# Written-out step lists for the first three batches and the last two in a five-engine software pipeline

## The chip, the cores and the metric

The kernel runs on one NeuronCore of a Trainium2 chip. The metric is the device time of one execution in microseconds (us), from its start to its end. Engines are named as in the profile: PE is TensorE, DVE is VectorE, ACT is ScalarE, POOL is GpSimd, SP is SyncE, whose queue issues most DMAs.

## The reference, cut to what matters

For each of 16 sequences ("batches") of 512 tokens with 128 channels the reference computes two layers. The first is an RWKV block and a soft decision tree:

```
x = ln(x); xn = ln(x); xk, xv, xr = mixes of xn and xn shifted by one token
k = exp(min(xk @ Wk, 60)); v = xv @ Wv; r = xr @ Wr
wk, wkv = scan over the tokens of k and k*v with a decay per channel
x = x + (sigmoid(r) * wkv / wk) @ Wo
x = x + sigmoid(xr2 @ cWr) + silu(xk2 @ cWk) @ cWv
x = ln(x); gates of 255 tree nodes; 256 leaf probabilities; x = ln(x + leaves @ values @ Wout)
```

The second is causal attention with 16 heads of 8 channels and rotary angles, and a mixture of 16 experts with the two largest gates, plus shared experts:

```
q, k = rope(rms(x) @ Wq), rope(rms(x) @ Wk); v = rms(x) @ Wv
x = ln(x + softmax(q k^T / sqrt(8), causal) @ v @ Wo)
x = ln(2 x + shared(x) + sum over the experts of gate_e * (x @ We))
```

The passes of one batch depend on one another nearly everywhere: time mix, channel mix, tree, rope, row maxima of the scores, scores and exponentials, attention output, routing, experts.

## The kernel before, in words

Every pass of a batch is cut into steps, each a few instructions of one engine with the semaphore waits that they need. In the file they are small functions: `row_scores` (steps `row0` to `row39`, PE), `row_maxima` (`rowmax0` to `rowmax39`, DVE), `scores` (`score0` to `score39`, PE), `score` (`exp0` to `exp39`, ACT), `weigh` (PE), `rope_product` (`rope0` to `rope3` on PE, `rope_mul0` to `rope_mul3` on DVE), `inverse` (DVE, the reciprocal of line 695), `read_out` (PE), `spread_gate` (`gb`), `expert` (PE), `gated_input` (`u`, even experts on DVE, odd ones on POOL, with ACT's `spread`).

A batch works in 40 score units. The row maxima come first: PE writes a unit into one of two PSUM banks, DVE reduces it (lines 745 and 748). When all are there, the maxima go through `max_parts`, a turn by PE and a DMA into extra rows of `qh`; then PE makes the units again, transposed and shifted by the maxima, and ACT takes the exponential (line 500). `prob` has ten slots; `weigh` frees them.

Rope's outputs are split into three bf16 parts each (`part_hi`, `part_mid`, `part_lo`). `spread_heads` (steps `heads0` and `heads1`, line 313) brings them by 18 DMAs for each half of the heads from `part` into `qh` and `kh`; `row0` of a batch waits for the first half.

Each engine runs in its own program order. The order is a hand-written cyclic list, `ORDER`: an entry `2:row5` in it means that in turn t the engine does `row5` of batch t-2. `run` repeats the list for turn 0, 1, 2 and so on, and leaves out what would fall on a batch below 0 or above 15. So at the start and at the end a turn has the same order as in the middle, with holes where there is no batch. A turn has the row maxima and the channel mix of one batch, the time mix of the next one, and the scores and experts of the one before.

Some constants are prepared inside batch 0's steps: the step `weights` on DVE (lines 854 to 902), PE (lines 1201 to 1206) and ACT (lines 615 to 623) scales, transposes and fuses weight matrices. PE's seventh transpose waits for DVE's first six instructions there, and all that PE has behind `weights`, `read_out0` of batch 0 first, waits for its end.

Two waits matter below. The time mix works in four chunks of 128 hidden channels with two slots of `rth` and `wkb`, so ACT's `r_tanh` of a chunk waits for POOL's `rwkv` of the chunk two before. And `read_out0` of a batch waits for `rwkv` of all four chunks, which follows `inverse3`.

## Time and profile before

| | |
|---|---|
| median of 3 runs | 1748.6 us (1747.52 to 1748.81) |
| profiled execution, its own time | 1748.68 us |
| its span, first to last instruction | 1746.5 us |
| PE busy | 1586.1 us, 91% |
| DVE busy | 1459.7 us, 84% |
| ACT busy | 1004.7 us, 58% |
| POOL busy | 911.6 us, 52% |
| mean granted TensorE clock | 0.965 |

The page is read in this order: the busy share of each engine, its course over 40 slices of the span, then the chain of work that ended last. A slice is 43.7 us. In the slices PE has 3, 4, 6, 6, 8 tenths at the start, then 9 without a break, and 8, 7, 6 at the end; DVE has 5, 6, 7, 6, 9 at the start and 8, 8, 3, 7, 1, 2 at the end. The work between the start and the end is the same in every turn, so the two ends are read by themselves, in windows.

### The profile page before, as it was taken

How to read it: one execution, taken by the hardware profiler on the slowest of the kernel's cores; microseconds unless marked ns; L12 is line 12 of the kernel's file. 1: busy time of each engine (PE TensorE's matmuls, PEld its weight loads, DVE VectorE, ACT ScalarE, POOL GpSimd, SP SyncE). 2: the span in 40 equal slices, each digit the busy share in tenths (PEclk: the TensorE clock that was granted, in tenths of full speed). 3: DMA queues.
4: the chain of work that ended last, by engine and by line, in shares of the span. 5: the costliest groups of instructions: out<-in, count | busy, mean ns of one | idle time of the engine just before them, and what ended most of it. 6: DMA issues, size and time to landing. Idle time of an engine off the chain costs nothing.

```text
span 1746.5 us, 33903 instructions
## 1 busy us (share of the span) xinstructions
PE 1586.1 (91%) x12128; PEld 1089.7 (62%) x12205; DVE 1459.7 (84%) x3450; ACT 1004.7 (58%) x2014; POOL 911.6 (52%) x1121
## 2 busy tenths in 40 slices
PE   3466899999999999999999999999999999999876
PEld 1334458576766758576766767576767767584735
DVE  5676989899898989899998989899998989883712
ACT  2243474756666574857566574757666565736261
POOL 6446174746556473846555474746455464632202
PEclk9687899999999999999999999999999999999897
DMA  4001020110102010100102020101102020201000
GB/s 109 0 7 55 8 56 8 33 30 17 52 8 56 15 55 8 45 24 24 46 8 62 9 55 8 53 17 31 39 10 59 9 56 2 61 3 53 10 14 7
DMA packets 66970, 53.36 MB, mean 31 GB/s; under 512 B 8370, under 2 KB 65522, under 8 KB 66802
## 3 DMA queue, kind: packets, MB, share of 16 engines
q1 hardware_dynamic: 65650, 50.41, 10.4%
q8 instruction: 96, 1.57, 0.4%
q10 hardware_dynamic: 1152, 0.79, 0.1%
q14 instruction: 72, 0.59, 0.1%
HBM read 8.44 MB, written 4.19 MB: 7 GB/s over the span
## 4 chain that ended last, share of the span: by engine, by line
PE 63%; DVE 20%; SPq 6%; ACT 5%; issue 4%; DMA 2%; POOL 1%; ACTq 0%; POOLq 0%; DVEq 0%; another core or an unknown queue 0%
PE bank L932 59%; DVE rmax L748 6%; SPq L313 5%; PE bank L928 4%; DMA kh<-part 2%; DVE inner L656 2%; DVE stats L647 2%; ACT prob L500 1%; DVE mixed L656 1%; DVE rmax L745 1%; DVE mv L652 1%; DVE xc L783 1%; ACT xbT L500 1%; ACT gT L500 0%; ACT part L500 0%
## 5 line engine op out<-in xcount | busy, mean ns | idle before, releaser
L500 ACT ACTIVATE prob<-bank 128x512 f32<-128x512 f32 x640 | 351.9, 601 | 170.1 <-PE bank L932 168.6
L748 DVE TENSOR_REDUCE rmax<-bank 128x1 f32<-128x512 f32 (+2 forms) x768 | 358.2, 504 | 49.8 <-PE bank L932 49.4
L446 POOL TENSOR_TENSOR prob<-xdT,spread 128x512 f32<-128x512 f32 x128 | 175.5, 1371 | 258.6 <-ACT spread L500 257.3
L932 PE MATMUL bank<-kh,qh 72*128 72x512 bf16 (+3 forms) x1024 | 252.5, 306 | 22.9 <-DVE rmax L748 9.9
L932 PE MATMUL bank<-wexpT,prob 128*128 128x128 f32 x2048 | 267.9, 276 | 3.1 <-issue 2.0
L932 PEld LDWEIGHTS bank<-wexpT,prob 128*128 128x128 f32 x2048 | 260.8, 192 | 11.4 <-issue 6.2
L932 PE MATMUL bank<-qh,kh 75*128 75x512 bf16 (+3 forms) x1024 | 242.8, 303 | 7.4 <-ACT prob L500 5.7
L695 DVE RECIPROCAL wkb<-wkb 128x512 f32<-128x512 f32 x64 | 213.7, 3340 | 0.0
L932 PE MATMUL bank<-maskb,identb 128*128 128x128 bf16 x1024 | 193.1, 222 | 0.0
L932 PE MATMUL bank<-maskTb,identb 128*128 128x128 bf16 x1024 | 191.2, 221 | 0.0
L500 ACT ACTIVATE spread<-bank 128x512 f32<-128x512 f32 x128 | 76.2, 596 | 185.5 <-PE bank L932 175.5
L932 PEld LDWEIGHTS bank<-qh,kh 75*128 75x128 bf16 x1024 | 100.2, 98 | 122.9 <-ACT prob L500 69.2
L932 PE MATMUL bank<-prob,vaug 128*32 128x512 f32 (+3 forms) x2048 | 163.0, 442 | 0.0
L390 POOL TENSOR_TENSOR wkb<-wkb,ksum 128x512 f32<-128x512 f32 x64 | 82.8, 1294 | 147.8 <-DVE ksum L682 121.7
L932 PEld LDWEIGHTS bank<-kh,qh 72*128 72x128 bf16 x1024 | 101.9, 100 | 88.0 <-DVE rmax L748 20.8
L500 ACT ACTIVATE rth<-bank 128x512 f32<-128x512 f32 x128 | 75.9, 593 | 77.8 <-PE bank L932 68.0
L932 PEld LDWEIGHTS bank<-maskTb,identb 128*128 128x128 bf16 x1024 | 101.1, 99 | 28.9 <-issue 25.2
L932 PEld LDWEIGHTS bank<-maskb,identb 128*128 128x128 bf16 x1024 | 102.2, 100 | 24.4 <-issue 15.9
L404 POOL TENSOR_TENSOR inner<-rth,wkb 128x512 f32<-128x512 f32 x64 | 109.1, 1704 | 11.5 <-DVE wkb L695 11.4
L360 POOL TENSOR_TENSOR rstd<-var,exponent 128x4 f32<-128x4 f32 x112 | 113.7, 1015 | 1.3
L932 PEld LDWEIGHTS bank<-prob,vaug 128*32 128x32 f32 x2048 | 54.6, 109 | 89.4 <-issue 51.2
L356 POOL TENSOR_TENSOR var<-mv,eps_ln 128x4 f32<-128x4 f32 x112 | 22.6, 201 | 165.6 <-DVE mv L652 165.6
(210 smaller groups left out, 3372.4 us busy)
## 6 DMA issues: line engine op xcount, KB each, us to landing
qh<-part SPq DMA_DIRECT2D x288, 64.0 KB
kh<-part SPq DMA_DIRECT2D x288, 64.0 KB
x<-in_L_attn_x_dram SPq DMA_DIRECT2D x16, 256.0 KB, 2.8
out_dram<-yo SPq DMA_DIRECT2D x16, 256.0 KB, 2.5
qh<-maxT SPq DMA_DIRECT2D x32, 24.0 KB
wk<-in_L_attn_tm_Wk_dram ACTq DMA_DIRECT2D x1, 256.0 KB, 5.8
wv<-in_L_attn_tm_Wv_dram ACTq DMA_DIRECT2D x1, 256.0 KB, 6.3
wr<-in_L_attn_tm_Wr_dram ACTq DMA_DIRECT2D x1, 256.0 KB, 6.6
```

Of the source, the lines that this page charges most:

```text
L313: sp.dma_start(dst[r:KROWS:PARTS * PARTS, z * NH // 2:(z + 1) * NH // 2, :], part[t][m][half, :]).then_inc(sems[("heads_low", "heads_high" ...
L360: raised(pool.tensor_tensor(rstd[:, n, :], var[:, n, :], exponent[:, :], ALU.pow), f"root{n}")
L390: raised(pool.tensor_tensor(wkb[:, c % 2, :], wkb[:, c % 2, :], ksum[:, c % 2, 0:T], ALU.add), "wk")
L404: raised(pool.tensor_tensor(inner[:, c, :], rth[:, c % 2, :], wkb[:, c % 2, :], ALU.mult), "rwkv")
L446: raised(pool.tensor_tensor(ug[:, e % 4, :], xdT[:, :], spread[e // 2 % 2][:, :], ALU.mult), "ug_side")
L500: raised(act.activation(dst, src, func, **kw), signal)
L647: last = dve.bn_stats(stats[:, n, j, :], t[:, j, :])
L656: return dve.scalar_tensor_tensor(out=out_, in0=in0, scalar=scalar, in1=in1, op0=op0, op1=op1)
L695: raised(dve.reciprocal(wkb[:, c % 2, :], wkb[:, c % 2, :]), "wk_inv")
L748: last = dve.tensor_reduce(rmax[:, j, h:h + 1], S[n % 2][:, col:col + (j + 1) * P], AX_X, ALU.max)
L928: last = pe.transpose(bk[:, j * P:(j + 1) * P], t[:, j, :], ident[:, :])
L932: return pe.matmul(out_, w, x, start=start, stop=stop, **kw)
```

## The change

Two tables are added beside `ORDER`, which stays as it is. `HEAD` writes out, for each engine, every step from the start up to a cut in the third turn; `TAIL` does so from a cut in the turn in which batch 14's row maxima are made to the end. `run` does the steps of `HEAD` in its order, then the cyclic list without any step that is in `HEAD` or `TAIL` (or was done before `run`), then the steps of `TAIL`. The steps themselves, their waits, tiles and DMAs are the same, and each is done once. Between the cuts each engine has the same steps in the same order as before. The cuts are, on PE, ahead of batch 0's `back1` (behind batch 1's `row0`) and ahead of batch 14's `row14`; on DVE, ahead of batch 1's `rowmax0` and ahead of batch 14's `rowmax12`. SP's list has the same order as before at both ends.

```diff
+HEAD = dict(
+    sp="""
+        0:load 0:shared_bias 1:load 0:heads0 0:heads1 2:load 0:max_rows0 0:max_rows1 1:heads0 1:heads1
+    """,
...
+TAIL = dict(
...
+    sp="""
+        14:max_rows0 14:max_rows1 12:store 15:heads0 15:heads1 15:max_rows0 15:max_rows1 13:store 14:store 15:store
+    """,
...
         def run(engine, steps, begun=()):
 
-            order = [(int(lag), name) for lag, name in (token.split(":") for token in ORDER[engine].split())]
+            order, first, last = ([(int(n), name) for n, name in (token.split(":") for token in table[engine].split())] for table in (ORDER, HEAD, TAIL))
+            placed = {*first, *last, *((0, name) for name in begun)}
+            for b, name in first:
+                steps[name](b)
             for turn in range(B + max(lag for lag, _ in order)):
                 for lag, name in order:
-                    if turn == lag and name in begun:
-                        continue
-                    if 0 <= turn - lag < B:
-                        steps[name](turn - lag)
+                    b = turn - lag
+                    if 0 <= b < B and (b, name) not in placed:
+                        steps[name](b)
+            for b, name in last:
+                steps[name](b)
```

In the lists of both ends an entry `1:row5` names the batch itself. In the rows below, the changed kernel's line numbers are higher by 120 for the same instruction, since the tables stand above it.

**Place 1: DVE, end of batch 0's time mix.** `kvb<-kvb,first,kvsum` is `wkv`, RECIPROCAL is `inverse`, `cwv` and `w_leaf` are the first and the last instructions of `weights`. Before, the last `wkv` and two `inverse` stand behind `weights`:

```order
L898 TENSOR_TENSOR part<-yo,part 1x512
L900 TENSOR_TENSOR w_leaf<-w_leaf,prob 128x256
L902 TENSOR_SCALAR w_leaf<-w_leaf 128x256
L656 SCALAR_TENSOR_TENSOR kvb<-kvb,first,kvsum 128x512
L695 RECIPROCAL wkb<-wkb 128x512 x2
L647 BN_STATS stats<-x_1 128x6 x4
```

In the change:

```order
L807 SCALAR_TENSOR_TENSOR kvsum<-decay,kvb 128x512
L815 RECIPROCAL wkb<-wkb 128x512
L776 SCALAR_TENSOR_TENSOR kvb<-kvb,first,kvsum 128x512
L815 RECIPROCAL wkb<-wkb 128x512
L974 TENSOR_SCALAR cwv<-cwv 128x512
L975 TENSOR_TENSOR prob<-prob 128x128
```

The two reciprocals moved ahead of `weights`. On ACT `weights` moved likewise, from ahead of `k_first3` to behind `r_tanh3`; on PE it stands behind `r3` in both.

**Place 2: DVE, end of batch 1's time mix and the start of batch 0's row maxima.** `tree<-cos_t,bank` and `tree<-sin_t,bank` are batch 0's `rope_mul` steps, `kk<-bank` is `clamp`, `ksum` and `kvsum` are the scans, `stats<-x_0` is the first norm of batch 2, `x<-x,bank` is `x2` of batch 1. Before:

```order
L695 RECIPROCAL wkb<-wkb 128x512
L739 TENSOR_TENSOR tree<-cos_t,bank 128x512
L739 TENSOR_TENSOR tree<-sin_t,bank 128x512
L695 RECIPROCAL wkb<-wkb 128x512
L647 BN_STATS stats<-x_0 128x6 x4
L652 BN_AGGR mv<-stats 128x2 x4
L705 TENSOR_TENSOR x<-x,bank 128x512
L647 BN_STATS stats<-x 128x6 x4
L652 BN_AGGR mv<-stats 128x2 x4
L748 TENSOR_REDUCE rmax<-bank 128x1 x6
```

In the change:

```order
L815 RECIPROCAL wkb<-wkb 128x512
L789 TENSOR_SCALAR kk<-bank 128x512
L859 TENSOR_TENSOR tree<-cos_t,bank 128x512
L776 SCALAR_TENSOR_TENSOR kvb<-kvb,first,kvsum 128x512
L859 TENSOR_TENSOR tree<-sin_t,bank 128x512
L795 TENSOR_TENSOR kvb<-kk,bank 128x512
L802 SCALAR_TENSOR_TENSOR ksum<-decay,kk 128x512
L815 RECIPROCAL wkb<-wkb 128x512
L807 SCALAR_TENSOR_TENSOR kvsum<-decay,kvb 128x512
L776 SCALAR_TENSOR_TENSOR kvb<-kvb,first,kvsum 128x512
L815 RECIPROCAL wkb<-wkb 128x512
L868 TENSOR_REDUCE rmax<-bank 128x1 x4
```

Batch 0's `rope_mul3` moved ahead of two reciprocals, and batch 0's row maxima follow the last reciprocal at once: `moments0` of batch 2 stands behind `rowmax2`, `x2` and `moments2` of batch 1 behind `rowmax7`. On PE batch 0's `rope2` and `rope3` stand ahead of batch 1's `r2` and `k3`, and `row0` to `row4` ahead of batch 1's `read_out0`.

**Place 3: DVE, last turn with row maxima (batch 15), beside the routing of batch 14.** `xc<-xc,bank` is `yc`, `lg<-bank,ebias` the first routing instruction. Before:

```order
L783 TENSOR_TENSOR xc<-xc,bank 128x512
L647 BN_STATS stats<-xc 128x6 x4
L652 BN_AGGR mv<-stats 128x2 x4
L748 TENSOR_REDUCE rmax<-bank 128x1 x6
L745 TENSOR_REDUCE rmax<-bank 128x2
L788 TENSOR_TENSOR lg<-bank,ebias 128x64
```

In the change:

```order
L903 TENSOR_TENSOR xc<-xc,bank 128x512
L767 BN_STATS stats<-xc 128x6 x4
L772 BN_AGGR mv<-stats 128x2 x4
L868 TENSOR_REDUCE rmax<-bank 128x1 x6
L865 TENSOR_REDUCE rmax<-bank 128x2
L868 TENSOR_REDUCE rmax<-bank 128x1 x6
L908 TENSOR_TENSOR lg<-bank,ebias 128x64
```

Nine units of maxima stand between `yc` and the routing instead of five. On PE the step `xdT` of batch 14 (the turn of the experts' input, which waits for ACT's `norm6`) stands behind `row11` instead of `row7`, and `centroids` behind `row13` instead of `row9`.

## Rows read from the trace of the kernel before

**Rows 1.** The page, part 4: the chain that ended last, by engine.

```profile
PE 63%; DVE 20%; SPq 6%; ACT 5%; issue 4%; DMA 2%; POOL 1%; ACTq 0%; POOLq 0%; DVEq 0%; another core or an unknown queue 0%
```

**Rows 2.** Busy us (count) by stretch: PE, PEld, DVE, ACT, POOL; clock, DMA share, GB/s.

```profile
250.13:1607.95 1357.82, 1324.42 (x10524) 923.03 (x10595) 1226.21 (x2922) 852.17 (x1705) 759.98 (x920) 1.00 0.11 31
104.29:147.20 42.91, 24.33 (x66) 11.30 (x65) 40.25 (x61) 14.12 (x24) 26.37 (x24) 0.82 0.04 11
155.60:206.20 50.60, 39.46 (x214) 23.01 (x212) 41.01 (x102) 19.61 (x39) 13.37 (x22) 0.83 0.10 27
206.20:250.10 43.90, 42.79 (x346) 24.46 (x346) 37.28 (x66) 33.34 (x66) 30.09 (x33) 0.96 0.11 30
1608.00:1660.30 52.30, 45.33 (x334) 36.35 (x339) 39.21 (x103) 13.91 (x30) 12.27 (x14) 0.84 0.08 23
1660.30:1694.00 33.70, 29.46 (x268) 13.45 (x266) 3.09 (x15) 23.45 (x43) 1.51 (x4) 0.95 0.03 10
```

**Rows 3.** Timeline (start, duration, what, [idle before <-releaser]): batch 0's constants and read-out.

```profile
52.66 0.40 DVE L854 TENSOR_SCALAR cwv<-cwv 128x512 f32<-128x512 f32 x1
62.17 6.56 DVE L695 RECIPROCAL wkb<-wkb 128x512 f32<-128x512 f32 x2
...
54.16 3.89 PE L1201 MATMUL bank<-ident,prob 128*128 128x128 f32 x17 [5.66 <-DVE prob L859]
59.43 0.96 PE L1206 MATMUL bank<-prob 128*128 128x128 f32 x4
70.17 5.54 PE L932 MATMUL bank<-wo,inner 128*128 128x128 f32 x32 [9.79 <-issue]
```

**Rows 4.** Timeline: batch 0's last rope product, first maxima, batch 1's read-out.

```profile
142.13 0.67 DVE L739 TENSOR_TENSOR tree<-sin_t,bank 128x512 f32<-128x512 f32 x1
142.72 3.35 DVE L695 RECIPROCAL wkb<-wkb 128x512 f32<-128x512 f32 x1
153.65 0.69 DVE L705 TENSOR_TENSOR x<-x,bank 128x512 f32<-128x512 f32 x1 [6.45 <-PE bank L932]
160.84 0.76 DVE L748 TENSOR_REDUCE rmax<-bank 128x1 f32<-128x384 f32 x2 [3.35 <-PE bank L932]
154.90 0.38 PE L932 MATMUL bank<-kh,qh 72*128 72x512 bf16 x1 [1.29 <-DMA kh<-part]
```

**Rows 5.** Groups of DVE instructions by line, 104 to 249 us.

```profile
L687 DVE TENSOR_TENSOR_SCAN kvsum<-decay,kvb 128x512 f32<-128x512 f32 x8 | 10.5, 1317 | 0.1
L669 DVE TENSOR_SCALAR kk<-bank 128x512 f32<-128x512 f32 x8 | 5.5, 688 | 4.0 <-PE bank L932 3.8
```

**Rows 6.** Timeline of PE: one projection of 512 columns, clock high and low.

```profile
106.86 1.12 PE L932 MATMUL bank<-mixed,wk 128*128 128x512 f32 x2
125.77 2.08 PE L932 MATMUL bank<-mixed,wk 128*128 128x512 f32 x2 [4.09 <-ACT rth L500]
```

**Rows 7.** Timeline of POOL: the same product beside DVE scans, and beside a reciprocal.

```profile
122.84 2.18 POOL L404 TENSOR_TENSOR inner<-rth,wkb 128x512 f32<-128x512 f32 x1
142.61 1.27 POOL L404 TENSOR_TENSOR inner<-rth,wkb 128x512 f32<-128x512 f32 x1
```

**Rows 8.** Timeline: batch 15's first row maxima, batch 14's route to the experts.

```profile
1607.95 0.39 PE L932 MATMUL bank<-kh,qh 72*128 72x512 bf16 x1 [0.39 <-DMA kh<-part]
1617.85 1.11 PE L928 MATMUL bank<-ident,xd 128*128 128x128 f32 x4 [2.32 <-ACT xd L510]
1619.64 0.76 DVE L748 TENSOR_REDUCE rmax<-bank 128x1 f32<-128x384 f32 x2 [3.35 <-PE bank L932]
1619.49 1.64 ACT L510 ACTIVATE xc<-xb,shift,rstd 128x128 f32<-128x128 f32 x4
```

**Rows 9.** Timeline of ACT: `spread` of batch 15's experts 3, 5 and 7.

```profile
1720.06 0.60 ACT L500 ACTIVATE spread<-bank 128x512 f32<-128x512 f32 x1 [2.71 <-PE bank L932]
1722.34 0.60 ACT L500 ACTIVATE spread<-bank 128x512 f32<-128x512 f32 x1 [1.68 <-PE bank L932]
1725.75 0.60 ACT L500 ACTIVATE spread<-bank 128x512 f32<-128x512 f32 x1 [2.81 <-PE bank L932]
```

105 lines of the change are left out of this document (added).

## The prediction

> **What bounds the kernel now.** I read the page's chain first, then busy time by stretch, then the timelines at both ends. The chain that ended last is PE for 63% and DVE for 20% [rows 1]: two engines take turns. The stretch from batch 1's `row0` to batch 15's is 14 turns of 97.0 us (1357.82 / 14), with PE busy 97.5% at a granted clock of 1.00 and DVE 90% [rows 2]. There the order is untouched by the change, and there is little to gain. What remains is 250.1 us ahead of it and 138.6 us behind it (1746.5 - 1607.95), where PE and DVE both have holes.
>
> **Head, batch 0's time mix (26 to 76 us).** DVE begins the constants at 52.66 and comes back to the two last reciprocals at 62.17, one `wkv` of 0.74 between; so the block takes 8.8 us, and they end at 68.73 [rows 3]. PE then has the read-out at 70.17, after 9.79 us idle. In the change the reciprocals come first and end near 68.7 - 8.8 = 59.9. DVE's part that PE needs is 54.16 - 52.66 = 1.5 us, PE's transposes and fusions take 60.39 - 54.16 = 6.2 [rows 3]: the read-out starts near 67.6, 2.6 us earlier, and it follows PE work directly instead of a long hole, so its 5.54 us should shrink, by the ratio of one projection at either clock (1.12 against 2.08 us [rows 6]) to 3.0 at best. I take 1.0 of these 2.5. Gain: **3.6 us**, with ends 2.0 (the changed order of clamp, scan and reciprocal brings in a wait) and 5.1. From there to batch 0's `y0` the chain is the same, step behind step.
>
> **Head, batch 1's time mix with batch 0's tree and rope (104.3 to 147.2).** DVE is busy 40.25 of 42.91 us [rows 2], so order cannot save much here; it decides what comes out first. In the change `moments0` (1.2 us) leaves this stretch, and three waits may come in: the tree is done sooner, so `rope_mul0` waits some 2 us for norm, turn and projection; `rope_mul1` waits about 1.3 and `clamp3` about 2.6, since PE must do `rope2`, `r2`, `rope3`, `k3` in a row between `rope_mul0` and `clamp3`, and at the low clock each is 2.08 us [rows 6], 8.3 together against some 5.7 of DVE work. So the last reciprocal ends 39.1 + 2.7 + 5.9 = 47.7 us after 104.3, at 152.0 in the old time scale, 6 later than before (142.72 + 3.35 = 146.07 [rows 4]). At the high clock these waits nearly vanish (four projections 4.5 us) and it ends near 146: both ends are kept.
>
> **But the maxima start at once.** Before, the first row maximum came at 155.6: `x2` stood before it, which waited 6.45 us for the read-out, and PE's `row0` waited for the heads' DMA until 154.90, 12.1 us after `rope_mul3` ended (142.80) [rows 4]. In the change six steps stand between `rope_mul3` and the last reciprocal's end, among them two reciprocals of 3.34 and a scan of 1.32 [rows 4, 5], 10.9 us in all, so it ends at 141.1; 12.1 later is 153.2, less where POOL and SP no longer hold batch 1's work in between. I take 152.5: a gain of **3.1 us**, ends 0 and 7.
>
> **The stretch of maxima (50.6 us before).** DVE was busy 41.01 of it [rows 2], the largest hole 3.35 where PE's rows stood behind a turn that waited for a norm [rows 4]. The change puts three steps of 3.1 us (`moments0`, `x2`, `moments2`) into it, and pushes three tree levels, two `kv`, one `clamp` and one `kvsum` behind it: 1.1 + 1.3 + 0.69 + 1.32 [rows 5] = 4.4. Busy becomes 39.7. Of 9.6 us idle I leave 4, because PE, busy 39.46 at a clock of 0.83 and now with batch 1's read-out too, is nearly as full as DVE. 43.7 against 50.6: **6.9 us**, ends 0 (PE stays at 1.2 GHz) and 10.9 (no idle at all).
>
> The granted clock in this stretch was 0.83 in the mean [rows 2], between the two levels of 1.2 and 2.4 GHz; the projection of 2.08 us ran at the low one after PE had waited 4.09 us [rows 6]. The Trainium skill ("TensorE: Matmul & The Clock Gate", section "What's actually happening") says that the throttled state is the default and that activity releases it. By that rule the denser stretch would run at 2.4 GHz throughout and my 6.9 would be nearer to 10; this is part of rival 2 below. The trace bears it out in the middle, where PE is busy 97.5% at 1.00.
>
> **The scores of batch 0 (43.9 us).** PE is busy 42.79 [rows 2]; it gets one more `v` (1.1 us) and DVE has the pushed 4.4 us to do before `x2` of batch 2. The last rope product keeps its distance to the start of this stretch, so the heads of batch 1 do too. Cost **1.0 us**, ends 0 and 3.
>
> POOL: the product of line 404 took 2.18 us beside DVE scans with two inputs and 1.27 beside a reciprocal [rows 7]. The skill ("SBUF — State Buffer", section "🔬 SBUF: two separate sides") calls the ports that DVE and GpSimd share an exclusive lock, with the loser blocked. By that rule packing DVE tighter would lengthen some of POOL's steps by 0.9 us each; it speaks against this change, by up to 4 us if four of them are on the path, which is less than the forecast's own range.
>
> Head: 3.6 + 3.1 + 6.9 - 1.0 = **12.6 us**.
>
> **Tail, up to batch 15's `row0`.** Batch 15's tree and rope come about 8 us earlier, but PE waited only 0.39 us for its heads [rows 8] and was otherwise full. Gain **0.4**, ends -1 and 2.
>
> **Tail, batch 15's maxima (52.3 us).** DVE is busy 39.21, PE 45.33 at a clock of 0.84 [rows 2]. `xdT` waited 2.32 us for ACT's norm with all rows behind it, and DVE stood 3.35 us [rows 8]. The change has four more units ahead of these waits, at some 0.7 us: 2.8. If the hole goes, so does part of the low clock after it; PE's 45.33 at 0.84 would be at most 7 us shorter at 1.00. I take 1.7 of it: **4.5 us**, ends 0 and 9.
>
> **Tail, scores and experts.** In the scores (33.7 us) ACT is busy 23.45 and PE 29.46 [rows 2]; three `weigh` in a row are split up, which may save 0.9, and ACT's `norm4`, 1.64 us [rows 8], moves from a hole beside the routing into the exponentials: half of it counts, 0.8. Among the last experts `spread` comes every 2.28 us, but one pair took 3.41 [rows 9], where two experts stood between two `gb` steps. The change gives one expert per `gb`: **1.1 us**. Sum 1.2, ends -1 and 3.
>
> Tail: 0.4 + 4.5 + 1.2 = **6.1 us**. All: 18.7 us, from 1748.68, the profiled execution's own time, to 1730.0. The median shown (1748.6) is the same within 0.1.
>
> **Rivals.**
> 1. *PE stays at 1.2 GHz in both stretches of maxima* (their clocks of 0.83 and 0.84 speak for it, their fuller order against). Head 3.6 + 3.1 + 1 - 1, tail 0.4 + 1 + 1.2: 9 us, **1740**.
> 2. *The clock stays high in the time mix too and the holes close*: head 5 + 7 + 10 - 1, tail 2 + 7 + 2: 32 us, **1717**.
> 3. *The head's gain is eaten between the cuts.* DVE reaches its cut about 1.5 us late against PE, because `x2` and `attend0` stand behind the pushed work. The middle order is the same, and its hole at `x2` (6.45 us in the head [rows 4]) should take this up in the first turn. If instead it does not, and each of the 14 turns of 97.0 us is longer, the price is 14 x 1.5 = 21 us: **1751**, slower. It decides from 1.34 us a turn. For it: PE has only 2.5% slack there [rows 2]. Against it: nothing in a turn can remember a late start but the waits themselves, and DVE has 10%.
> 4. *Both ends are bound by one batch's own chain*, so the order matters only where work of another batch stood in front: 1.0 + 0 + 2 - 1 in the head, 1 in the tail: about **1746**, within 0.2%.
>
> That the lists do not do what they say is hardly possible: the steps are the same set, once each, and the middle is the old order.
>
> **How the numbers follow.** A measurement of this kernel can tell some 0.2%, 3.5 us, from no change. Forecast (1721 to 1736): 0.58. Rival 1 (1736 to 1744): 0.17. Rival 2 (below 1721): 0.13. Rival 4: 0.05. Rival 3: 0.07. Faster is the first three, 0.88; same 0.05; slower 0.07. The range goes from 1716 to 1743: it takes in most of rivals 1 and 2 and leaves out some 15 in 100.
>
> **What would show it.** Batch 0's read-out starts near 67.6 us. Its first row maximum comes near 149 (152.5 less 3.6) instead of 155.6, and the stretch to the first score unit takes 43 to 45 us. Batch 1's `row0` stands near 237 instead of 250.1, and batch 15's 1357 to 1359 us behind it. Batch 15's maxima take some 48 us; no pair of `spread` takes over 2.5 us. Wrong would be: a clock under 0.8 from 150 to 195 us; a first row maximum later than 153; or a middle longer than 1360.

## The result, and the profile after

The changed kernel takes **1729.53 us** in the median of 4 runs (1728.1 to 1730.45), the kernel before 1748.7 us beside it (1747.52 to 1750.76). The ratio is 0.9889, with a 95% interval of 0.9873 to 0.9904: about 19 us, or 1.1%, faster. The profiled execution took 1729.01 us, with a span of 1726.7 us.

The page of the changed kernel: busy time, the two rows of slices that matter here, and the chain that ended last, to set against [rows 1].

```profile
PE 1590.5 (92%) x12205; PEld 1087.3 (63%) x12205; DVE 1463.2 (85%) x3450; ACT 1006.8 (58%) x2014; POOL 913.2 (53%) x1121
...
PE   3467999999999999999999999999999999999976
...
PEclk9786999999999999999999999999999999999897
...
PE 64%; DVE 19%; SPq 6%; ACT 5%; issue 3%; DMA 2%; POOL 1%; ACTq 0%; DVEq 0%; POOLq 0%
```

The shares hardly moved: the gain is at the ends, and the middle is as it was. Busy time by stretch in the changed kernel, in the columns of [rows 2]: batch 1's time mix, batch 0's maxima, batch 0's scores, the middle (from batch 1's `row0` to batch 15's), batch 15's maxima, batch 15's scores.

```profile
97.07:141.30 44.23, 25.54 (x77) 12.70 (x77) 40.55 (x53) 14.61 (x25) 28.17 (x25) 0.81 0.11 30
141.30:191.90 50.60, 45.35 (x238) 28.65 (x236) 40.60 (x107) 19.49 (x39) 16.60 (x28) 0.75 0.10 27
191.90:239.30 47.40, 44.73 (x349) 23.68 (x348) 42.40 (x77) 34.69 (x67) 31.52 (x32) 1.00 0.10 27
239.38:1592.96 1353.58, 1328.83 (x10595) 922.34 (x10595) 1226.25 (x2922) 853.72 (x1705) 759.35 (x919) 1.00 0.11 31
1592.96:1643.28 50.32, 45.92 (x342) 37.15 (x339) 38.75 (x98) 12.75 (x26) 13.67 (x17) 0.83 0.08 23
1643.28:1676.00 32.72, 28.46 (x270) 12.90 (x269) 4.22 (x21) 25.11 (x47) 1.51 (x4) 1.00 0.03 10
```

The second line is the surprise: the maxima of batch 0 took 50.60 us, exactly as long as before [rows 2], with PE busy for 45.35 of them instead of 39.46, and the clock at 0.75 instead of 0.83. To see where the gain was made, I take the start of the same instruction in both traces and subtract (us):

| from ... to | before | after | gain | predicted |
|---|---|---|---|---|
| start ... `x2` of batch 0 | 75.75 | 68.40 | 7.35 | 3.6 |
| ... first row maximum of batch 0 | 79.83 | 72.91 | 6.92 | 3.1 |
| ... its first score on PE | 50.76 | 50.94 | -0.18 | 6.9 |
| ... `yc` of batch 1 | 146.33 | 149.72 | -3.39 | -1.0 |
| ... `yc` of batch 12 (11 turns) | 1072.30 | 1072.10 | 0.20 | 0 |
| ... `row0` of batch 15 | 182.98 | 178.89 | 4.09 | 0.4 |
| ... `yd` of batch 14 (behind batch 15's maxima) | 52.33 | 50.32 | 2.01 | 4.5 |
| ... `yd` of batch 15 | 78.18 | 75.36 | 2.82 | 1.2 |
| ... end of the span | 8.09 | 8.09 | 0 | 0 |

The gains add up to 19.8 us. The head gave 10.7 (I said 12.6), the tail 8.9 with what lies ahead of `row0` (I said 6.1). `yc` is the sum of attention and its input, on DVE, one per batch; it is the best marker of a turn. In the changed kernel two of them are 97.4 us apart.

The head of the changed kernel, timeline: last reciprocal of batch 0, two of the constants' instructions with what POOL does beside them, the read-out, `x2`.

```profile
53.45 3.35 DVE L815 RECIPROCAL wkb<-wkb 128x512 f32<-128x512 f32 x1
...
56.88 1.31 POOL L524 TENSOR_TENSOR inner<-rth,wkb 128x512 f32<-128x512 f32 x1 [0.77 <-DVE wkb L815]
56.99 1.35 DVE L975 TENSOR_TENSOR prob<-prob 128x128 f32<-128x128 f32 x1
...
64.63 3.74 PE L1052 MATMUL bank<-wo,inner 128*128 128x128 f32 x32
...
68.40 0.69 DVE L825 TENSOR_TENSOR x<-x,bank 128x512 f32<-128x512 f32 x1 [1.21 <-PE bank L1052]
```

The last reciprocal ended at 56.8 (53.45 + 3.35) instead of 68.73, and the read-out began at 64.63 instead of 70.17 and took 3.74 us instead of 5.54 [rows 3]. Then the maxima, timeline: first row maximum, the read-out of batch 1 on PE between the rows, and DVE's hole behind it; last, PE's hole, in which DVE does `x2` and its statistics.

```profile
141.31 2.19 DVE L868 TENSOR_REDUCE rmax<-bank 128x1 f32<-128x512 f32 x4 [0.26 <-PE bank L1052]
...
144.18 3.73 PE L1052 MATMUL bank<-wo,inner 128*128 128x128 f32 x16
...
148.47 1.40 DVE L868 TENSOR_REDUCE rmax<-bank 128x1 f32<-128x512 f32 x3 [2.54 <-PE bank L1052]
...
154.10 0.39 PE L1052 MATMUL bank<-kh,qh 72*128 72x512 bf16 x1 [2.06 <-DVE rmax L868]
```

Sixteen products of the read-out took 3.73 us here; all 32 of batch 0 had taken 3.74. The granted clock was 0.50 from 141 to 147 us, its lower level of 1.2 GHz, right behind PE's wait for the heads (it stood 8.59 us ahead of `row0`), and 1.00 in batch 0's read-out. DVE stood 2.54 us behind the slow products. My theory from here on: **the clock is what kept the predicted 6.9 us away.** The rival: the holes come from the order of PE's steps and DVE's waits, and a lower clock only makes PE look busier.

### The profile page after: what moved, and what is told of

Same layout as the page of the kernel before. It is cut to its first block, busy times and chain, and to the rows that moved or that the text cites. A ratio compares the mean times of both kernels' runs of the same rounds, so it can differ in the third digit from the quotient of the medians.

```text
span 1726.7 us, 33980 instructions
## 1 busy us (share of the span) xinstructions
PE 1590.5 (92%) x12205; PEld 1087.3 (63%) x12205; DVE 1463.2 (85%) x3450; ACT 1006.8 (58%) x2014; POOL 913.2 (53%) x1121
## 4 chain that ended last, share of the span: by engine, by line
PE 64%; DVE 19%; SPq 6%; ACT 5%; issue 3%; DMA 2%; POOL 1%; ACTq 0%; DVEq 0%; POOLq 0%
PE bank L1052 60%; DVE rmax L868 5%; SPq L433 5%; PE bank L1048 4%; DMA kh<-part 2%; DVE inner L776 2%; ACT prob L620 2%; DVE stats L767 2%; DVE mixed L776 1%; DVE rmax L865 1%; DVE mv L772 1%; DVE wkb L815 1%; DVE xc L903 1%; ACT xbT L620 0%; ACT part L620 0%
## 5 line engine op out<-in xcount | busy, mean ns | idle before, releaser
L524 POOL TENSOR_TENSOR inner<-rth,wkb 128x512 f32<-128x512 f32 x64 | 105.1, 1643 | 9.2 <-DVE wkb L815 8.3
L953 DVE TENSOR_TENSOR prob<-xdT,bank 128x512 f32<-128x512 f32 x128 | 87.0, 680 | 21.5 <-PE bank L1052 21.5
```

The source lines that it names most:

```text
L524: raised(pool.tensor_tensor(inner[:, c, :], rth[:, c % 2, :], wkb[:, c % 2, :], ALU.mult), "rwkv")
L953: raised(dve.tensor_tensor(ug[:, e % 4, :], xdT[:, :], G, ALU.mult), "ug")
```

## The experiments

The runs were made in three groups, each with the kernel before beside it, whose median was 1751.1, 1748.8 and 1750.3 us. So a time's distance to the change is read best from the ratio to before; the interval of a ratio is some 0.1 to 0.3% to either side. Where a part is under 5 us, I go by the times within the trace. A trace is one execution: single turns of the middle differ by up to 1.3 us from run to run, and the stretches of maxima by more (last section), and both are in the spans. The table has starts in us.

| kernel | `x2`(0) | row max(0) | score(0) | `yc`(1) | `yc`(12) | `yc`(15) | span |
|---|---|---|---|---|---|---|---|
| before | 75.75 | 155.58 | 206.34 | 352.67 | 1424.97 | 1697.40 | 1746.5 |
| the change | 68.40 | 141.31 | 192.25 | 341.97 | 1414.07 | 1678.30 | 1726.7 |
| head_only | 69.45 | 142.57 | 193.52 | 343.67 | 1415.64 | 1687.04 | 1735.5 |
| tail_only | 75.71 | 156.12 | 206.94 | 352.78 | 1424.65 | 1688.68 | 1737.2 |
| constants_first | 73.96 | 146.96 | 197.87 | 348.03 | 1421.04 | 1685.19 | 1733.0 |
| place_one_only | 69.55 | 149.76 | 201.04 | 346.96 | 1419.90 | 1683.56 | 1731.8 |
| fill_row0 | 68.97 | 141.67 | 187.83 | 337.94 | 1410.33 | 1672.60 | 1720.8 |
| fill_head | 68.92 | 141.62 | 184.89 | 336.07 | 1409.65 | 1673.29 | 1721.1 |
| fill_tail | 68.71 | 141.64 | 192.58 | 342.21 | 1415.37 | 1678.26 | 1726.9 |
| constants_later | 72.93 | 145.42 | 196.35 | 346.24 | 1419.25 | 1682.97 | 1731.1 |
| constants_split | 68.30 | 144.13 | 190.57 | 340.25 | 1413.10 | 1675.14 | 1723.4 |
| best | 68.47 | 143.53 | 186.84 | 336.46 | 1408.93 | 1670.53 | 1719.0 |
| tail_rows_old | 68.00 | 140.85 | 191.79 | 341.62 | 1413.39 | 1680.93 | 1729.5 |
| fill_old | 76.02 | 155.66 | 203.00 | 349.69 | 1422.92 | 1693.73 | 1742.9 |

### Are the two ends independent? head_only and tail_only

```diff
-TAIL = dict(sp="12:store ...", pool="...", act="...", dve="...", pe="...")
+TAIL = dict(sp="", pool="", act="", dve="", pe="")      # head_only; tail_only does the same to HEAD
```

Expected for head_only:

> The list for the head stays, the list for the tail is empty, so batch 15's last passes go in the cyclic order. Theory (the two ends are independent, and the middle carries the head's gain unchanged): the added result of batch 1's attention came 10.7 us earlier in the change and that of batch 12 still 10.9, so this kernel takes 1748.7 - 10.8 = 1737.9 us, and its last passes after row0 of batch 15 take the 138.6 us of before. Rival (the new tail is what lets the head's gain through, since the old tail is bound by something of its own): 1742 or more.

Measured: 1736.43 us (1732.45 to 1740.02), ratio 0.9916 (0.989 to 0.9942); its profiled run has a span of 1735.5. `yc`(1) came 9.0 us earlier than before, after a start that was 1.05 us later than in the change (`x2`(0)), and `yc`(12) 9.3 earlier. From `yc`(12) to `yc`(15) it took 271.4 us, before 272.4, the change 264.2. By the ratio the head's list is worth 14.7 us, with an interval of 10.1 to 19.2; by `yc`(1) and the span of this one trace, 9.0 and 11.0. The rival's 1742 is out.

Expected for tail_only:

> The list for the head is empty, the list for the tail stays. Theory (independent ends): the tail gains what the head does not, 19.2 - 10.8 = 8.4 us, so 1740.3 us, and of it 3.5 us lie ahead of row0 of batch 15, where my prediction had 0.4. Rival (row0 of batch 15 came earlier only because the head's gain reached it in another phase): row0 of batch 15 stays at 1607 to 1608 us and the time is 1744 or more.

Measured: 1742.19 us (1739.43 to 1743.5), ratio 0.9952 (0.9934 to 0.9969), which is 8.4 us of 1748.7. `row0` of batch 15 came at 1603.34, 178.7 us behind `yc`(12), against 178.9 in the change and 183.0 before: the rival is out. The two ends are independent and the middle carries what the head gained. By the starts in the traces the head's list is worth 9 to 11 us and the tail's some 9; the whole times agree with that within their intervals, but are too wide to say it alone. PE's idle time ahead of `row0` of batch 15 shrank where the new list takes tree, rope and `weigh` in other places: in the 84.7 us before it PE was idle 4.4, in the change's 81.5 it was 2.5, and its waits for a `prob` of ACT fell from 2.5 to 1.5 us. Which of these moves does most of the 4.1 us was not tried.

### What is place 1 worth? constants_first and place_one_only

```diff
 # constants_first, HEAD of dve (act: 0:weights back behind 0:k_exp3)
-0:ksum3 0:kvsum3 0:inverse2 0:wkv3 0:inverse3 0:weights 1:moments0
+0:ksum3 0:kvsum3 0:weights 0:inverse2 0:wkv3 0:inverse3 1:moments0
```

> The changed kernel with one thing put back: VectorE's and ScalarE's block of constants of batch 0 stands ahead of the last two reciprocals again (the order of scans and reciprocals stays new). Theory (the block is on the only path of batch 0, and everything behind hangs on it): read-out of batch 0 near 67 us instead of 64.6, at the low clock again (5.5 us instead of 3.7), x2 of batch 0 near 72.5 instead of 68.4, and the whole kernel 4 us slower than the change, 1733.6. Rival (later waits, the heads' transfers and the maxima, absorb it): x2 late by as much, but the end within 1 us of the change, 1729.5 to 1730.5.

Measured: 1734.4 us (1728.82 to 1735.73), ratio 0.9903 (0.9882 to 0.9924). `x2`(0) at 73.96 and `yc`(1) at 348.03, 5.6 and 6.1 us behind the change, where 4 was expected, and in this trace nothing later took it up (`yc`(15) is 6.9 behind). So the theory held in the trace. The whole time is less sharp: the loss is 2.4 us by the ratios and 4.9 by the medians, and the fastest of the four runs is no slower than the change. Timeline of constants_first: the same VectorE instruction as above, and the read-out.

```profile
51.40 0.28 DVE L974 TENSOR_TENSOR prob<-prob 128x128 f32<-128x128 f32 x1
...
58.98 3.35 DVE L814 RECIPROCAL wkb<-wkb 128x512 f32<-128x512 f32 x1
...
67.60 6.32 PE L1051 MATMUL bank<-wo,inner 128*128 128x128 f32 x32 [9.74 <-issue]
```

The read-out follows 9.74 us without work and takes 6.32 us at a clock of 0.58, against 3.74 at 1.00 when it follows the constants' matmuls directly. So nearly half of what this place is worth is the clock: 3.0 us of start, 2.6 of duration. The other 1.8 us of the 7.35 (75.75 to 73.96) are the new order of clamps, scans and reciprocals, which my sum had at nothing. (`x2`(0) by itself lies between 68.00 and 69.55 in the change and the six kernels of the table that share its start of the head, so these figures are good to some 1.5 us.)

place_one_only keeps the new head up to the end of the constants and has the old order from there to the cut:

```diff
 # HEAD of dve behind 0:weights; pe, act and pool in the same way
-1:moments0 0:x2 0:moments2 1:moments1 0:mix3 0:mix4 0:silu0 ...
+1:moments0 0:x2 0:moments2 0:mix3 0:mix4 0:silu0 0:silu1 1:moments1 ...
```

> The changed kernel, with the head's list kept only up to the end of batch 0's constants, and the order of before from there to the cut; the tail's list stays. Theory (gains add up: x2 of batch 0 is 7.35 us earlier by this part, the rest of the head adds 10.8 - 7.3 = 3.5 net): 1729.5 + 3.5 = 1733 us; the stretch from the first row maximum of batch 0 to its first score unit stays 50 to 51 us. Rival (the old order of batch 1's time mix and maxima loses the early start in the wait for the read-out, so the later part is worth nearly all of the head's gain): 1737 to 1740.

Measured: 1734.16 us (1732.54 to 1736.25), ratio 0.9908 (0.9893 to 0.9924). From `x2`(0) to `yc`(1) it took 277.4 us; before 276.9, the change 273.6. So place 1 goes straight through, and all the rest of the head's new order is worth 3.8 us, as the theory had it (3.5). It looked like far more: the first row maximum is 7.3 us nearer to `x2`(0) in the change (72.9 against 80.2). But then 0.3 are gained in the maxima and 3.8 lost in the scores. Work that had stood ahead of the first row maximum, above all batch 1's read-out, now stands behind it.

### Is it the clock? fill_row0 and fill_head

Matmuls of constants into a bank that nobody reads keep PE busy where it would wait. They add work and take none away.

```diff
+            def fill(b, count):
+                for _ in range(count):
+                    mm((T1 if b else O)[:, 0:P], wk[:, 0:P], wk[:, 0:P])
 # HEAD of pe
-1:r3 0:row0 0:row1
+1:r3 0:fill32 0:row0 0:row1
 # fill_head also: 0:fill8 0:row10, 0:fill4 2:xnT, 0:fill2 0:row28, 0:fill1 0:row30, 0:fill1 1:xbT
```

> The changed kernel, with 32 matmuls of 128 columns added on TensorE ahead of row0 of batch 0, into a bank that nobody reads, so that TensorE is busy for most of the 8.6 us in which it waits for the heads' transfer. Theory (the holes of VectorE behind the first row maximum are TensorE's low clock, which follows from that idle time): the granted clock from 141 to 147 us is 1.00 instead of 0.50, read_out of batch 1 has no 2.5 us hole of VectorE behind it, and the stretch of maxima takes 48 us instead of 50.6. Rival (the holes are the order of PE's steps, and the clock only adds to PE's busy time): the clock rises, the stretch stays at 50 to 51 us.

Measured: 1722.76 us (2 runs), ratio 0.985 (0.983 to 0.987). The stretch took 46.2 us, less than the 48 expected. Its windows, and the read-out with the row maximum behind it:

```profile
135.00:141.00 6.00, 4.87 (x44) 4.67 (x42) 5.96 (x4) 0.00 (x0) 6.00 (x6) 1.00 0.36 100
141.00:147.00 6.00, 5.15 (x31) 4.14 (x32) 5.00 (x16) 0.00 (x0) 5.62 (x10) 0.72 0.36 101
152.00:157.00 5.00, 3.67 (x19) 2.17 (x20) 4.40 (x13) 3.67 (x10) 4.60 (x7) 0.62 0.05 13
```

```profile
144.33 3.00 PE L1051 MATMUL bank<-wo,inner 128*128 128x128 f32 x16
...
147.65 1.35 DVE L867 TENSOR_REDUCE rmax<-bank 128x1 f32<-128x512 f32 x3 [1.60 <-PE bank L1051]
```

The clock was 0.72 in the mean from 141 to 147, where 1.00 was expected and the change had 0.50, so the read-out is only partly faster (3.00 instead of 3.73) and the hole shrank to 1.60, not to none. It fell again behind PE's next wait (0.62 from 152 to 157). The expectation had the direction and the mechanism, but not the windows.

> As before, and fillers also ahead of row10, row28 and row30 of batch 0, of batch 2's first turn and batch 1's turn for the tree (16 more matmuls of 128 columns, in holes of TensorE of 2.1, 0.9, 0.6 and 0.25 us). Theory (low clock is what keeps my predicted 6.9 us away): the granted clock is over 0.95 from 141 to 192 us, the stretch takes 44 to 46 us, and the kernel gains 3 to 5 us, 1725 to 1727 beside 1729.5 for the change. Rival (DVE, busy 40.6 of 50.6 us, and its waits for norms set the pace): stretch 49 us or more, total within 1 us of the change; or, if fillers come late, slower.

Measured: 1722.99 us (1722.55 to 1724.01), ratio 0.9852 (0.9837 to 0.9867). The stretch, in the columns of [rows 2]:

```profile
141.60:184.60 43.00, 39.95 (x270) 27.63 (x268) 40.07 (x108) 19.49 (x39) 16.88 (x28) 0.96 0.12 33
```

This settles the question. PE, with the fillers in it, is busy 39.95 us instead of 45.35, DVE does its 40.07 us in 43.0 instead of 50.6, at a clock of 0.96. The order of steps and their waits are those of the change, and fillers only add work, so nothing but the clock can have made the stretch shorter. The rival said 49 or more. My predicted 43.7 us for this stretch was what the new order can do at the high clock; the order alone does not bring the clock. One part of the rival stays: DVE's hole behind batch 1's read-out is 1.59 us here too. The Trainium skill ("TensorE: Matmul & The Clock Gate", section "What's actually happening") has the throttled state as the default, released by activity. The traces agree: in the change PE was idle ahead of `row0` and the clock was 0.50 from 141 to 147 us; with the fillers ahead of it, it was 0.72 there.

A trace without any filler says the same. constants_split (below) has the change's order from `row0` to the first score, and in its traced execution, the fastest of its four, the clock came back earlier:

```profile
144.13:190.57 46.44, 40.83 (x238) 25.78 (x237) 40.67 (x109) 19.46 (x39) 16.70 (x28) 0.84 0.11 29
```

It took 46.4 us at 0.84, with PE 10.11 us idle ahead of `row0`, while the change and five other kernels with this order and no filler in this stretch took 50.9 at 0.75 or 0.76. So what fill_row0 shows in its trace an execution can also get by chance; what the fillers add is that all six runs of fill_row0 and fill_head are at 1722.6 to 1724.0 us.

The total is that of fill_row0 all the same. It was 2.9 us ahead at the first score and 1.9 at `yc`(1); from there to `yc`(12) it took 1073.6 us against 1072.4, and batch 15's maxima took 49.4 against 48.2, at clocks of 0.86 and 0.93.

### Does the old order lack it too? fill_old

```diff
 # the old order of pe, written out
+0:fill32 1:read_out0 ... 0:fill5 0:row0 ... 0:fill8 1:xn2T ... 0:fill4 2:xnT ... 0:fill2 1:xbT
```

> The kernel before (its order written out for the head), with fillers on TensorE of batch 0: 32 ahead of batch 1's read-out (7.0 us idle), 5 ahead of row0, 8 ahead of the turn for batch 1's channel mix (2.3 us idle), 4 and 2 ahead of two later turns. Theory (the clock that falls in TensorE's holes costs either order about the same): the read-out takes 3.7 us instead of 6.1, the stretch of maxima 46 us instead of 50.6, and the kernel 5 to 7 us less than before, 1742 to 1744. Rival (in the old order TensorE waits for norms and VectorE anyway, and the clock is not what it lacks): 1746 to 1749.

Measured: 1745.24 us (1741.86 to 1748.25, 10 runs), ratio 0.9973 (0.9962 to 0.9983). `yc`(1) came 3.0 us earlier than before, the maxima took 47.3 us instead of 50.8. The theory had 5 to 7 us, the rival up to 2.7; by the ratio it is 4.7 (3.0 to 6.6), by `yc`(1) 3.0, so it lies between them. In the timeline of fill_old batch 1's read-out takes 3.84 us instead of 6.12, and then DVE waits for other things than the clock:

```profile
147.80 3.84 PE L1008 MATMUL bank<-wo,inner 128*128 128x128 f32 x32
...
151.68 0.69 DVE L781 TENSOR_TENSOR x<-x,bank 128x512 f32<-128x512 f32 x1 [4.19 <-PE bank L1008]
...
155.66 2.19 DVE L824 TENSOR_REDUCE rmax<-bank 128x1 f32<-128x512 f32 x4 [1.98 <-PE bank L1008]
...
160.95 0.76 DVE L824 TENSOR_REDUCE rmax<-bank 128x1 f32<-128x384 f32 x2 [3.09 <-PE bank L1008]
```

The first row maximum stayed at 155.66, because it waits for the heads' transfer, and the hole of 3.09 us behind the norm stayed too. In these traces `yc`(1) gains 5.9 us from 48 fillers in the new order and 3.0 from 51 in the old one, so order and clock seem to help each other; with one trace of each that is not shown.

### The tail's maxima: fill_tail and tail_rows_old

```diff
 # TAIL of pe (fill_tail)
+15:fill5 15:row7  15:fill1 15:row8  15:fill1 15:row9  15:fill1 15:row10  15:fill1 15:row11 ... 15:fill8 15:row17
```

> The changed kernel with 17 fillers of 128 columns in the tail only: 5 ahead of row7 of batch 15 (TensorE stood 1.17 us there), one each ahead of row8 to row11, 8 ahead of row17 (2.0 us hole). Theory (my term of 4.5 us for batch 15's maxima came out at 2.0 because the clock fell to 0.50 from 1603 to 1620 us): the clock is 1.00 throughout, the stretch from row0 to yd of batch 14 takes 46 us instead of 50.3, and the kernel 1725.5. Rival (the stretch is bound by batch 14's own chain of norms and routing, and by VectorE's row maxima): 49.5 us or more, the kernel 1729 to 1730.

Measured: 1727.12 us (1725.22 to 1728.96), ratio 0.9875 (0.986 to 0.989). The stretch from `row0` to batch 14's `yd`:

```profile
1594.25:1643.24 48.99, 45.64 (x367) 38.57 (x373) 38.67 (x98) 12.50 (x26) 13.67 (x17) 0.93 0.08 23
```

The clock rose from 0.83 to 0.93, and the stretch fell only from 50.3 to 49.0 us, where I had expected 46. Here the rival is nearly right: PE still stood 2.07 us for a row maximum behind the routing, whose nineteen short DVE instructions stood before it, and the clock fell once more behind that wait (0.65 from 1612 to 1618 us). But this comparison cannot credit the fillers. Eight kernels, the change among them, have the same tail without them, and in their traces the stretch varies by itself with the clock; fill_row0, then constants_split:

```profile
1589.38:1637.58 48.20, 41.53 (x337) 33.93 (x339) 38.68 (x99) 12.74 (x26) 13.67 (x17) 0.93 0.08 24
```

```profile
1591.70:1640.11 48.41, 41.75 (x337) 33.99 (x339) 38.67 (x98) 12.73 (x26) 13.64 (x17) 0.93 0.09 24
```

For the other six it is 49.4 to 50.3 us at 0.83 to 0.86. So 0.83 to 0.93 is worth 1.3 to 2.1 us in this stretch, and the gain of fill_tail by its fillers is not shown.

```diff
 # tail_rows_old: PE and DVE from batch 15's row0 to its score0 in the old order
-15:row11 14:xdT 15:row12 15:row13 14:centroids        # pe
+15:row7 14:xdT 15:row8 15:row9 14:centroids
-14:moments6 15:rowmax5 ... 15:rowmax13 14:route_logits # dve
+14:moments6 15:rowmax5 ... 15:rowmax9 14:route_logits
```

> The changed kernel, with TensorE and VectorE back in the old order from row0 of batch 15 to its score0 (batch 14's turn for the experts behind row7 again, five units of maxima between yc and the routing); all else stays. Theory (the wider distance between yc and the routing is what gained 2.0 us there): VectorE has its 3.35 us hole again, this stretch takes 52.3 us instead of 50.3, and the kernel 1731.5. Rival (the gain in that stretch came from elsewhere, from work that had left it): 50.3 us, 1729.5.

Measured: 1730.62 us (2 runs), ratio 0.9894 (0.9874 to 0.9913), which does not tell it from the change. The trace does: `row0` at 1592.62 and batch 14's `yd` at 1645.90, 53.3 us against 50.3 (which is the most in the eight traces with the new tail), and `yc`(12) to `yc`(15) took 267.5 against 264.2. The hole is back where it had been in [rows 8]; tail_rows_old first, then the change at the same place:

```profile
1599.48 1.92 DVE L867 TENSOR_REDUCE rmax<-bank 128x1 f32<-128x512 f32 x4
1604.77 0.75 DVE L867 TENSOR_REDUCE rmax<-bank 128x1 f32<-128x384 f32 x2 [3.37 <-PE bank L1051]
```

```profile
1599.80 2.68 DVE L868 TENSOR_REDUCE rmax<-bank 128x1 f32<-128x512 f32 x6
...
1605.31 1.40 DVE L868 TENSOR_REDUCE rmax<-bank 128x1 f32<-128x512 f32 x3 [0.63 <-PE bank L1052]
```

### Can the constants leave the path? constants_later and constants_split

```diff
 # constants_later, HEAD of pe
-0:weights 0:read_out0 0:read_out1 0:read_out2 0:read_out3 0:xn2T
+0:read_out0 0:read_out1 0:read_out2 0:read_out3 0:weights 0:xn2T
```

> The changed kernel with TensorE's part of the constants moved one place further: behind the four steps of batch 0's read-out instead of ahead of them. Theory (the constants stand on the path only because the read-out waits behind them): the read-out starts near 58.5 us instead of 64.6, at the low clock (5.5 us), x2 comes near 64 instead of 68.4, ScalarE's norm for the channel mix, which stands behind its part of the constants, near 69.5 instead of 72.1, and the kernel is 2.5 us faster than the change, 1727. Rival (the norm is held up by the constants on ScalarE by as much as the read-out gained): norm at 72, the time of the change.

Measured: 1733.25 us (1732.11 to 1734.17), ratio 0.991 (0.9893 to 0.9926), slower than the change. The read-out began at 58.83 as expected, and took 6.53 us after 11.76 us without work. But `x2` was far from 64:

```profile
58.83 6.53 PE L1051 MATMUL bank<-wo,inner 128*128 128x128 f32 x32 [11.76 <-POOL inner L523]
...
71.07 0.42 DVE L1019 TENSOR_TENSOR w_leaf<-w_leaf,prob 128x256 f32<-128x256 f32 x1 [5.84 <-ACT w_leaf L742]
...
72.93 0.66 DVE L824 TENSOR_TENSOR x<-x,bank 128x512 f32<-128x512 f32 x1
```

I had looked at what is queued behind the constants on ScalarE and not on VectorE: `x2` stands behind the leaf weights there, and these wait for PE's part. constants_split was made for that:

```diff
 # HEAD of dve
-0:inverse2 0:wkv3 0:inverse3 0:weights 1:moments0 0:x2 0:moments2
+0:scaled 0:inverse2 0:wkv3 0:inverse3 0:weights 1:moments0 0:x2 0:moments2 0:biases
```

> The changed kernel with VectorE's block of constants cut in three: the six scalings that TensorE's transposes need (1.5 us) ahead of the last two reciprocals, the rope weights behind the last reciprocal, the biases and the leaf weights behind x2 and its statistics. constants_later had put x2 at 72.9, because the leaf weights stood ahead of x2 on VectorE and waited for TensorE. Theory: transposes run while TensorE is idle, read-out of batch 0 at 60 us on a high clock (3.7 us), x2 at 63.5 to 64 instead of 68.4, the whole kernel 4 to 4.5 us faster than the change, 1725. Rival (the biases now stand ahead of the channel mix on VectorE and give half of it back): x2 at 64, result of the channel mix only 2 us earlier, 1727.5.

Measured: 1728.74 us (1725.51 to 1730.63), ratio 0.9881 (0.9866 to 0.9896): no difference from the change that could be told; the traced execution is the fastest, 1725.51, by the clock in its two stretches of maxima (above). `x2`(0) came at 68.30, not at 63.5. Timeline:

```profile
60.52 1.26 POOL L523 TENSOR_TENSOR inner<-rth,wkb 128x512 f32<-128x512 f32 x1 [0.77 <-DVE wkb L814]
60.57 1.29 DVE L987 COPY w_rope<-prob 128x64 f32<-128x64 f32 x1
...
61.89 6.37 PE L1055 MATMUL bank<-wo,inner 128*128 128x128 f32 x32 [3.13 <-issue]
```

The read-out began 2.7 us earlier than in the change and took 2.6 us longer: PE had stood 3.13 us, and that gave the gain back. In the change the constants that stand in the read-out's way are also what keeps the clock up for it. Both theory and rival of this run had `x2` wrong. What the rival feared is there all the same: the biases and leaf weights now stand between `x2` and the channel mix, and its result (`x<-thr,bank`) came at 90.80 us, 1.9 later than in the change, the first row maximum 2.8 later.

### All together: best

constants_split with the fillers of fill_head and fill_tail.

> constants_split with the fillers of fill_head and of fill_tail together. Theory (the three effects are in different places and add up): 4.4 for the constants, 6.5 for the head's fillers, 1.3 for the tail's, 1729.5 - 12.2 = 1717.3 us. Rival (the earlier start moves the stretches against the fillers, whose number was set for the old positions, or the heads' transfers become the bound): 1720 to 1722.

Measured: 1721.45 us (1720.9 to 1724.97), ratio 0.9848 (0.9832 to 0.9864), 0.4% under the change. The parts did not add up to 1717, which leaves the rival's 1720 to 1722: constants_split was worth nothing of its 4.4; the maxima took 43.3 us in the head and 47.8 (clock 0.96) in the tail. fill_row0 (0.985), fill_head (0.9852) and this one cannot be told apart: one row of 32 fillers ahead of `row0` does nearly all of it.

## Why the prediction was right, and where it was not

1730.0 was forecast and 1729.5 measured. What held is the frame: both ends gain, they are independent, and the middle carries the head's gain. That the sum came out within 0.5 us is luck: of its eight terms only the middle's zero was near, three were 2.4 to 7.1 us too high, and four were 1.6 to 3.8 us too low.

- **Batch 0's time mix, 3.6 us: measured 7.35.** The place of the constants was worth 5.6 (constants_first), 3.0 by an earlier start and 2.6 by the clock. I had the read-out's 5.54 us shrink by 1.0; it shrank by 1.8. The step that failed is "they end near 68.7 - 8.8 = 59.9": they ended at 56.8. The new order of clamp, scan and reciprocal, which I took for a possible wait, gained 1.8 us instead.
- **Batch 1's time mix and the first row maximum, +3.1: measured 6.9.** I had the last reciprocal 5.9 us late from three waits. It ended at 141.05, 44.0 us behind the first clamp at 97.07, where 47.7 was forecast. `rope_mul0` waited 1.11 and `rope_mul1` 0.88 us; `clamp3` waited for nothing worth a line. And `row0` came 10.8 us behind `rope_mul3` (129.77 to 140.58), sooner than "12.1 later". "Near 149" was 141.31.
- **The stretch of maxima, 6.9: measured -0.2.** This is the failed step that matters: "of 9.6 us idle I leave 4", with PE "nearly as full as DVE". DVE's busy time was well forecast (39.7, measured 40.6). PE's was not: the read-out moved in, the clock fell to 0.75 in the mean, and PE was busy 45.35 us. This was my own lower end ("0, PE stays at 1.2 GHz"), and rival 1's mechanism, in the head. fill_head shows that the clock kept it away: 43.0 us against 43.7. The sign that I had set for this, "a clock under 0.8 from 150 to 195 us", missed it: the clock there was 0.81, and before it had been 0.78; the low stretch began at 141.
- **The scores of batch 0, -1.0: measured -3.4.** This stretch took 47.4 us where it had been 43.9, at a clock of 1.00, PE busy 44.7 instead of 42.8 and DVE 42.4. With more of batch 2's time mix and batch 1's tree behind the maxima both engines have more to do here. The cost's ends of "0 and 3" were too narrow, and batch 1's `row0` came at 239.4 instead of "near 237".
- **The middle, 0.** `yc`(1) to `yc`(12) took 1072.1 us, before 1072.3. Rival 3 (1.5 us more a turn) did not happen, and head_only and tail_only show the ends to be independent.
- **Tail ahead of `row0`, 0.4: measured 4.1.** I saw PE "otherwise full" there. It was idle 4.4 of 84.7 us and is now idle 2.5 of 81.5; its busy time fell too, from 80.3 to 79.0, as the clock of 0.98 became 1.00. I had read the clock from the stretch as a whole and not ahead of `row0`.
- **Batch 15's maxima, 4.5: measured 2.0.** The hole went from 3.35 us to pieces of 0.63 and 0.87, and was priced well at 2.8: 2.0 against before, 3.0 against tail_rows_old. The clock did not follow, 0.83 where it had been 0.84. That is the 1.7 "of it": the size fits what 0.93 is worth in other traces (1.3 to 2.1 us, fill_tail), but closing the hole did not bring that clock in the change.
- **Scores and experts, 1.2: measured 2.8.** Of that 2.1 are the scores. The claim "no pair of `spread` takes over 2.5 us" was wrong for the first: they start at 1697.64 and 1701.08, 3.44 us apart, all others within 2.9; what [rows 9] shows moved rather than went.
- **POOL's ports.** The prediction feared up to 4 us from POOL's steps beside DVE. In batch 0's constants it is DVE that paid: see below. What POOL paid in the whole was not measured.

Rival 2 (clock high everywhere, 1717) was not what the change does, but is what it leaves: the kernel best comes to 1721.

## What to carry to other kernels

Where work is moved so that an engine's rows come earlier, ask at which clock PE will run them: the same 16 products took 3.73 us behind an idle stretch, while 32 took 3.74 without one, so a stretch can keep its length though its idle time on paper has gone. Matmuls that compute nothing, in the waits ahead of such a stretch, gave 6.8 us of 1729 for 32 short instructions, and setup work can play the same part, if it is put in front of the work that needs the clock. Two traces of one order can differ by 4.5 us in one stretch through the clock alone, so a small gain in one trace is no gain until other runs show it. And a sum of terms that comes out right shows nothing about its terms: mark the same instruction of each stage in both traces and subtract, before believing any of them.

## What the hardware showed that was not expected

**A short DVE instruction can wait for a product of POOL.** In the change `prob<-prob` of line 975, 128 columns, started at 56.99 and took 1.35 us, ending just behind POOL's product (56.88 to 58.19). In constants_first the same instruction took 0.28 us. In constants_split a copy of 64 columns took 1.29 us beside POOL's 1.26, where its equals take 0.20 or 0.21. Reciprocals of 3.35 us ran through beside such products. The Trainium skill ("SBUF — State Buffer", section "🔬 SBUF: two separate sides") has the shared ports as an exclusive lock for the whole instruction, taken by DVE where it has two inputs in SBUF or runs a mode with two ports; these rows agree.

**The heads' transfer differs from run to run.** PE's waits for it from 260 to 1600 us, one per batch (total, count, longest), least in tail_only and most in constants_first; before had 6.5 us, the change 5.4 and fill_head 6.4:

```profile
PE bank L1015 <- DMA kh<-part: 4.7, 13, 0.7
```

```profile
PE bank L1051 <- DMA kh<-part: 7.1, 13, 1.2
```

Most turns take 97.4 us, single ones 97.6 to 98.6, and in fill_head the longer turn I looked at (531 to 629 us) has `row0` wait 1.2 us for it, the next one less than that. But these waits look too small to be why runs of one kernel differ by up to 8 us: between these traces they differ by 2.4 us over thirteen turns, and in all traces the eleven turns from `yc`(1) to `yc`(12) differ by 1.8 us.

**Where runs of one kernel differ, the granted clock mostly differs with them.** In fill_old, with ten runs, the four fastest (1741.9 to 1743.5 us) have mean clocks of 0.971 to 0.973, the four slowest (1746.8 to 1748.3) 0.966 to 0.969. In constants_first the run at 1728.82 has 0.970, the three at 1733.7 to 1735.7 have 0.964 or 0.965. In the traces the same steps took 46.4 us at 0.84 and 50.9 at 0.75 in batch 0's maxima, 48.2 at 0.93 and 50.3 at 0.83 in batch 15's. In place_one_only and constants_later, whose runs differ by 3.7 and 2.1 us, the mean clocks show nothing of it. What lets the clock come back earlier in one execution than in the next stays open, and so does why the transfers differ.
